# First layer's experts by unordered pairs: one sorted row a token, two experts a block

## The reference

```python
logits = xn @ gate_w + gate_b
tw, ti = jax.lax.top_k(logits, K)            # K = 2 of E = 6 experts
tw = jax.nn.softmax(tw, axis=-1)
w_full = jnp.sum(tw[..., None] * jax.nn.one_hot(ti, E, dtype=tw.dtype), axis=-2)
h = jax.nn.gelu(einsum('bsd,edh->besh', xn, ew1) + eb1, approximate=False)   # H = 256
eo = einsum('besh,ehd->besd', h, ew2) + eb2
moe = einsum('bse,besd->bsd', w_full, eo)
abel = gelu(xn @ aw1 + ab1) @ aw2 + ab2      # 128 -> 512 -> 128
nonabel = moe rotated by four expm(gens[i])
gate = sigmoid(concat([abel, nonabel]) @ gc_w + gc_b)
g = x + abel * (1 - gate) + nonabel * gate
```

## Time and profile before

| | us |
|---|---|
| median of 3 runs | 713.91 |
| lowest, highest | 711.11, 715.43 |
| the profiled execution | 718.61 |
| its span, first to last instruction | 716.9 |
| PE busy in the span | 626.8 |
| DVE busy | 496.5 |
| ACT busy | 415.2 |
| POOL busy | 447.6 |

### The profile page before, as it was taken

One profiled execution on the slowest core, in us unless ns is written; L12 is line 12 of the kernel. 1 busy time (PEld: TensorE's weight loads), 2 busy tenths in 40 slices (PEclk: granted clock), 3 DMA queues, 4 the chain that ended last, 5 costly groups with the idle time before them and its releaser, 6 DMA issues.

```text
span 716.9 us, 19568 instructions
## 1 busy us (share of the span) xinstructions
PE 626.8 (87%) x6221; PEld 443.8 (62%) x6222; DVE 496.5 (69%) x1302; ACT 415.2 (58%) x1144; POOL 447.6 (62%) x663
## 2 busy tenths in 40 slices
PE   4799889786876997896799999995999999999994
PEld 3667767686875865675354555554999845555442
DVE  5678776667665716998488888883444477887884
ACT  2575334443443454776666787773444367878793
POOL 7775888887068869974122476764333258878782
PEclk9999999999999999998999999998999999999997
DMA  8995111144566621110010000001222101111110
GB/s 230 289 301 149 42 45 56 56 113 87 104 114 127 128 56 33 31 24 13 1 32 2 8 32 24 24 28 35 69 70 70 56 21 42 32 32 31 32 46 16
DMA packets 69466, 48.34 MB, mean 67 GB/s; under 512 B 8011, under 2 KB 63750, under 8 KB 69382
## 3 DMA queue, kind: packets, MB, share of 16 engines
q1 hardware_dynamic: 62332, 34.09, 18.4%
q0 software_dynamic: 6144, 12.63, 7.3%
q10 hardware_dynamic: 906, 0.55, 0.3%
HBM read 24.00 MB, written 23.24 MB: 66 GB/s over the span
## 4 chain that ended last, share of the span: by engine, by line
PE 41%; POOL 23%; issue 17%; DVE 8%; DMA 5%; ACT 3%; SPq 1%; DVEq 0%; ACTq 0%; POOLq 0%
PE bank L1746 6%; PE bank L1817 5%; PE bank L1826 5%; POOL vs L1658 5%; POOL pool_xy L1056 5%; PE bank L1012 4%; DMA xg<-x_half 4%; PE bank L1726 3%; POOL xn_all L1634 3%; PE bank L1115 2%; POOL spacer L1051 2%; PE bank L1125 2%; DVE nmx L2058 2%; PE bank L579 2%; PE bank L1105 1%
## 5 line engine op out<-in xcount | busy, mean ns | idle before, releaser
L1891 ACT ACTIVATE pb<-bank,nmx 128x512 f32<-128x512 f32 x256 | 173.5, 691 | 65.5 <-DVE nmx L2058 62.6
L2058 DVE TENSOR_REDUCE nmx<-bank 128x2 f32<-128x1024 f32 x128 | 155.1, 1215 | 13.3 <-PE bank L1746 11.8
L1227 ACT ACTIVATE turns<-bank,cols 128x128 f32<-128x128 f32 x148 | 46.4, 364 | 65.5 <-PE bank L1115 41.4
L1658 POOL TENSOR_TENSOR vs<-vt_first,rz 128x256 f32<-128x256 f32 x64 | 39.4, 615 | 70.9 <-DVE rz L2034 69.9
L1726 PEld LDWEIGHTS bank<-pb,vs 128*32 128x32 f32 x2048 | 54.5, 110 | 37.6 <-issue 19.4
L1726 PE MATMUL bank<-pb,vs 128*32 128x128 f32 x2048 | 69.6, 275 | 2.0 <-POOL vs L1658 2.0
L382 POOL DMA_INDIRECT x_half<-pool_xy,slot x64 | 62.3, 973 | 10.6 <-issue 10.6
L1746 PE MATMUL bank<-qk 64*128 64x512 f32 x256 | 65.6, 622 | 1.6 <-ACT pb L1891 1.1
L1746 PE MATMUL bank<-qk_first 64*128 64x512 f32 x256 | 64.6, 619 | 2.2 <-ACT pb L1891 1.0
L1658 POOL TENSOR_TENSOR vs<-vt,rz 128x256 f32<-128x256 f32 x64 | 39.2, 615 | 36.5 <-DVE rz L2034 32.1
L1691 POOL COPY xn_all<-w 128x512 f32 x39 | 23.9, 615 | 51.3 <-PE bank L1817 49.2
(11 more groups left out here) (275 smaller groups left out, 1450.6 us busy)
## 6 DMA issues: line engine op xcount, KB each, us to landing
y_half<-ys SPq DMA_DIRECT2D x74, 64.5 KB
x_half<-zero SPq DMA_DIRECT2D x2, 2368.0 KB, 17.6
xg<-x_half SPq DMA_DIRECT2D x74, 64.0 KB
x_sorted<-zero SPq DMA_DIRECT2D x1, 2496.0 KB, 18.5
xn_all<-x_sorted SPq DMA_DIRECT2D x39, 64.0 KB, 1.8
y_sorted<-xn_all SPq DMA_DIRECT2D x39, 64.0 KB, 1.6
x_all<-in_L_attn_x_dram SPq DMA_DIRECT2D x8, 256.0 KB, 6.8
w<-in_L_ffn_W_dram SPq DMA_DIRECT2D x1, 2048.0 KB, 11.9
```

The costliest lines, as they stand in the source:

```text
L1658: pool.tensor_tensor(vs[s][:, :, :], vt[bt % 2][:, n // 2 % TT, :, :].rearrange("p j d -> p (j d)") .unsqueeze(1).broadcast_to([P, 2, D]), ...
L1891: act.activation(pb[s + ab][:, :], psum[score_banks(k) + ab], ACT.Exp, bias=nmx[:, s + ab:s + ab + 1], scale=1.0, accum_out=zz[:, s + ab:s ...
L2058: dve.tensor_reduce(nmx[:, s:s + 2], banks[:, score_banks(k):score_banks(k) + 2, :], AX.X, ALU.max, negate=True).then_inc(n_mx, 1)
```

## The change

A token has one class instead of two experts: the unordered pair of its experts, NC = 15. Each token is sorted once, into NB0 = 32 + 14 = 46 blocks; its row in the table is 130 wide, the 128 values and the two weights. DVE makes the classes as products of the two-hot rows, over all tokens at once: `ranks`, `offsets`, `first_blocks` and `slots` run once, in batches 4 and 5, on 15 x 32 = 480 values instead of twice on 96, and `block_experts` makes two expert numbers a block in batches 5 and 6. The two weights come from an exponential of ACT (`pair_weights`). POOL scatters 32 times, once the numbers, the weights and the zero fill are there. In a block, PE does four first and four second products, ACT four gelus, POOL (no longer DVE) copies the first weights of both experts, and DVE puts both biases, each scaled by its weight, into the result and adds both experts' halves out of the bank by their weights. In the mixing one row a token is gathered, all 32 behind the last block; the residual is added by DVE's first pass of `mix`, the dense part by its second, straight out of the banks, and ACT's `first_part` and POOL's `residual` are gone. In the second layer the scatters go one in two steps.

```diff
 NTH = NT // 2
-NBH = 2 * NTH + E0 - 1
-NB0 = 2 * NBH
+NC = E0 * (E0 - 1) // 2
+NB0 = NT + NC - 1
...
     def scatter(g):
-        for slot_w in (slot1, slot2):
-            pool.indirect_dma_start(
-                out=x_half[g // NTH], out_offset=bass.IndirectOffsetOnAxis(ap=slot_w[:, g:g + 1], axis=0),
-                in_=xh[:, g, :], in_offset=None).then_inc(t_sc0[g // NTH], 16)
-            space()
+        pool.indirect_dma_start(
+            out=x_pair, out_offset=bass.IndirectOffsetOnAxis(ap=slot0[:, g:g + 1], axis=0),
+            in_=xh[:, g, :], in_offset=None).then_inc(t_sc0, 16)
+        space()
...
-    for h in range(2):
-        pool.wait_ge(a_sl, h + 1)
-        pool.wait_ge(t_zf[h], 16)
-        for g in range(h * NTH, (h + 1) * NTH):
-            scatter(g)
+    pool.wait_ge(a_wt, 2)
+    pool.wait_ge(a_sl, 1)
+    pool.wait_ge(t_zf[0], 16)
+    for g in range(NT):
+        scatter(g)
...
-        dve.tensor_tensor(mo[:, :, :], oh1[:, half, :], oh2[:, half, :], ALU.add).then_inc(a_mo, 1)
...
+        dve.tensor_tensor(sg[:, half], sn[:, half], mt[:, :], ALU.is_gt)
+        step(dve.tensor_tensor(mo[:, :, :], oh1[:, half, :], oh2[:, half, :], ALU.add))
+        for a in range(E0 - 1):
+            n = E0 - 1 - a
+            last = dve.tensor_tensor(cls[:, FIRST_OF[a]:FIRST_OF[a] + n, half],
+                                     mo[:, :, a + 1:E0].rearrange("p t e -> p e t"),
+                                     mo[:, :, a].unsqueeze(1).broadcast_to([P, n, NTH]), ALU.mult)
+        last.then_inc(a_mo, 1)
...
+            dve.tensor_tensor(wp[:, :], sg[:, :], u[:, :], ALU.mult)
+            step(dve.tensor_tensor(wq[:, :], sn[:, :], v[:, :], ALU.mult))
+            dve.tensor_tensor(xh[:, :, D + i], wp[:, :], wq[:, :], ALU.add).then_inc(a_wt, 1)
+            dve.wait_ge(a_wt, i + 1)
...
-        for oh, slot_w in ((oh1, slot1), (oh2, slot2)):
-            step(dve.tensor_tensor(offo[:, :, :], off0[:, :, :], oh[:, half, :].rearrange("p t e -> p e t"),
-                                   ALU.mult))
-            step(dve.tensor_reduce(sl_f[:, :], offo[:, :, :].rearrange("p e t -> p t e"), AX.X, ALU.add))
-            last = dve.tensor_copy(slot_w[:, half], sl_f[:, :])
-            if oh is oh1:
+        step(dve.tensor_tensor(offo[:, :, :], off0[:, :, :], cls[:, :, :], ALU.mult))
+        step(dve.tensor_reduce(sl_f[:, :], offo[:, :, :].rearrange("p c t -> p t c"), AX.X, ALU.add))
+        dve.tensor_copy(slot0[:, :], sl_f[:, :]).then_inc(a_sl, 1)
...
             norm(1)
-        if bt - 1 in ROUTES:
-            slots(ROUTES.index(bt - 1))
+        if bt == ROUTES[1] + 1:
+            slots()
+            pair_weights()
         if bt in ROUTES:
             first_pick(ROUTES.index(bt))
...
+        both = expert(k)
+        if k >= NW:
+            pool.wait_ge(o_up, k - NW + 1)
+        for i in range(2):
+            pool.tensor_copy(wst0[k % NW][:, i * H0:(i + 1) * H0],
+                             w_e1[:, bass.ds(both[i], 1), :].rearrange("p a h -> p (a h)")).then_inc(o_w, 1)
+    def gather(g, alone=False):
+        pool.indirect_dma_start(
+            out=yg0[:, g, :], out_offset=None, in_=y_pair,
+            in_offset=bass.IndirectOffsetOnAxis(ap=slot0[:, g:g + 1], axis=0)).then_inc(f_yg[g // TT], 16)
+        if not alone:
             space()
...
-    for g in range(4):
-        gather(NTH + g)
-    for bt in range(1, B + 2):
-        first = 4 + (0, 2, 4, 6, 8, 9, 11)[bt - 1] if bt < B else NTH
-        if bt <= B:
-            residual(bt - 1)
-        if first < NTH:
-            gather(NTH + first)
-        if 2 <= bt:
-            power(bt - 2)
-        if first + 1 < NTH and bt != 5:
-            gather(NTH + first + 1)
+    for j in range(NY):
+        pool.wait_ge(o_st[j], 16 * ((NB0 - 1 - j) // NY + 1))
+    for g in range(2 * TT):
+        gather(g)
+    for bt in range(2, B + 2):
+        if bt < B:
+            gather(bt * TT)
+            gather(bt * TT + 1, True)
+        power(bt - 2)
+        if bt < B:
+            gather(bt * TT + 2)
+            gather(bt * TT + 3)
...
     def expert_down(k):
...
+        both = expert(k)
         pe.wait_ge(o_h, k + 1)
         if k > 1:
             pe.wait_ge(o_y, k - 1)
...
+        for i in range(2):
+            for c in range(EC):
+                mm = pe.matmul(psum[MBANK[k % 2]][:, i * DX:(i + 1) * DX],
+                               hT0[k % NW][:, (i * EC + c) * P:(i * EC + c + 1) * P],
+                               w_e2[:, bass.ds(both[i] * EC + c, 1), :].rearrange("p a d -> p (a d)"),
+                               start=(i == 0 and c == 0), stop=(c == EC - 1), skip_group_check=True)
...
-        if n == 2 and bt > 2:
+        if n == 3 and bt > 2:
             next_T(bt - 3)
         down(c)
-        if n == 3 and bt > 2:
-            next_scores(bt - 3)
+        if n == 0 and bt > 3:
+            next_scores(bt - 4)
+    next_scores(B - 4)
...
         gelu(bt * AC + 1)
+        if bt:
+            gate_tanh(bt - 1)
+        gelu(bt * AC + 2)
         if bt > 1:
             silu_tanh(bt - 2)
-        if bt:
-            gate_tanh(bt - 1)
...
-        gelu(bt * AC + 2)
         gelu(bt * AC + 3)
+        if bt + 1 < B:
+            gelu(bt * AC + 4)
         if bt > 2:
             next_store(bt - 3)
...
     def store_turned(k):
         dve.wait_ge(o_T, k + 1)
-        if 1 < k <= LEAD:
+        if k > 1:
             dve.wait_ge(o_up, k - 1)
...
+    def first_bias(k):
+        if k >= NY:
+            dve.wait_ge(o_st[k % NY], 16 * (k // NY))
+        dve.tensor_scalar(ys0[k % NY][:, :], bias_of(expert(k)[0]), weight_of(k, 0), None, ALU.mult).then_inc(o_b1, 1)
+    def second_bias(k):
+        dve.wait_ge(o_b1, k + 1)
+        dve.scalar_tensor_tensor(ys0[k % NY][:, :], bias_of(expert(k)[1]), weight_of(k, 1), ys0[k % NY][:, :],
+                                 ALU.mult, ALU.add).then_inc(o_b2, 1)
+    def first_expert(k):
         dve.wait_ge(o_dn, k + 1)
-        if k >= NB0 - LEAD:
-            dve.wait_ge(o_st[k % NY], 16 * (k // NY))
-        dve.tensor_tensor(ys0[k % NY][:, :], psum[MBANK[k % 2]][:, 0:DX],
-                          b2x[:, bass.ds(e, 1), :].rearrange("p a d -> p (a d)"), ALU.add).then_inc(o_y, 1)
-    copy_weight(0)
+        dve.wait_ge(o_b2, k + 1)
+        dve.scalar_tensor_tensor(ys0[k % NY][:, :], psum[MBANK[k % 2]][:, 0:DX], weight_of(k, 0), ys0[k % NY][:, :],
+                                 ALU.mult, ALU.add).then_inc(o_f1, 1)
+    def second_expert(k):
+        dve.wait_ge(o_f1, k + 1)
+        dve.scalar_tensor_tensor(ys0[k % NY][:, :], psum[MBANK[k % 2]][:, DX:2 * DX], weight_of(k, 1), ys0[k % NY][:, :],
+                                 ALU.mult, ALU.add).then_inc(o_y, 1)
...
     for i in range(NB0 + LEAD):
-        expert(i + 2)
+        expert(i)
+        if 0 <= i - 2 < NB0:
+            first_bias(i - 2)
         if i < NB0:
             store_turned(i)
-        if i + 1 < NB0:
-            copy_weight(i + 1)
         if i >= LEAD:
-            finish_block(i - LEAD)
-    dve.wait_ge(f_th, 1)
-    dve.tensor_scalar(w2t[:, :], th[:, :], 0.5, 0.5, ALU.mult, ALU.add)
-    step(dve.tensor_scalar(w1t[:, :], th[:, :], -0.5, 0.5, ALU.mult, ALU.add))
+            first_expert(i - LEAD)
+        if 0 <= i - 2 < NB0:
+            second_bias(i - 2)
+        if i >= LEAD:
+            second_expert(i - LEAD)
...
+        dve.wait_ge(f_yg[bt], 16 * TT)
+        if bt:
+            dve.wait_ge(f_gt, bt)
         dve.wait_ge(f_dn, (bt + 1) * AC)
-        dve.tensor_tensor(gz[:, 0:3], gz[:, 0:3], a[:, 0:3 * DX].rearrange("p (t d) -> p t d", t=3)[:, :, D], ALU.add)
-        dve.tensor_tensor(gz[:, 3:4], gz[:, 3:4], b_[:, D:DX], ALU.add).then_inc(f_gz, 1)
...
+        dve.tensor_tensor(gz[:, 0:3], yg0[:, bt * TT:bt * TT + 3, D],
+                          a[:, 0:3 * DX].rearrange("p (t d) -> p t d", t=3)[:, :, D], ALU.add)
+        dve.tensor_tensor(gz[:, 3:4], yg0[:, bt * TT + 3, D:DX], b_[:, D:DX], ALU.add).then_inc(f_gz, 1)
...
-        dve.wait_ge(f_r0, bt + 1)
+        a, b_ = (psum[i] for i in ABANKS[bt % 2])
+        dve.wait_ge(f_gg, bt + 1)
+        dve.wait_ge(f_xa, bt + 1)
         for t in range(TT):
-            y = in_half(bt * TT // NTH, bt * TT + t)
-            ins = dve.scalar_tensor_tensor(r[:, t, :], y[:, 0, 0:D], gw1[:, t:t + 1], r[:, t, :], ALU.mult, ALU.add)
+            ins = dve.scalar_tensor_tensor(r[:, t, :], yg0[:, bt * TT + t, 0:D], gg[bt % 2][:, t:t + 1],
+                                           xn_all[:, bt * TT + t, :], ALU.mult, ALU.add)
         step(ins)
         for t in range(TT):
-            y = in_half(bt * TT // NTH, bt * TT + t)
-            ins = dve.scalar_tensor_tensor(r[:, t, :], y[:, 1, 0:D], gw2[:, t:t + 1], r[:, t, :], ALU.mult, ALU.add)
+            mine = a[:, t * DX:t * DX + D] if t < 3 else b_[:, 0:D]
+            ins = dve.scalar_tensor_tensor(r[:, t, :], mine, og[bt % 2][:, t:t + 1], r[:, t, :], ALU.mult, ALU.add)
```

(22 more changed lines are left out.)

288 lines of the change are left out of this document (135 added, 153 removed).

## The result

| | before | with the change |
|---|---|---|
| median, us | 714.67 (4 runs, 711.11 to 716.12) | 741.12 (4 runs, 737.61 to 744.82) |
| the profiled execution, us | 718.61 | 737.61 |
| its span, us | 716.9 | 735.9 |

The ratio is 1.0357, with a 95% interval of 1.0306 to 1.0407: the change costs 3.6%, and the forecast of 741.0 lies on the median. (The forecast started from 713.9, the median of three of these four runs of the kernel before.) How much of that is luck the stages tell. The execution profiled with the change lies 3.5 under its median, the one of before 3.9 over its own, so the two traces are only 19.0 us apart and not 26.5.

A forecast was written before the change was run, and what follows sets the result against it. No engine was full in the experts' stretch; scatters and the mixing's chain were the other places to see. Start +14.9, blocks −7.9, mixing +22.8, second layer −3.0: +26.8 on 713.9 gives 741, range 733 to 750.

The forecast's parts named there:

- Start of the blocks: Scatters and POOL's queue ahead of the experts' stretch: PE's first product at 155.4 instead of 140.51, +14.9 us.
- its cover: What the routing adds to the attention, some 7 us at most, hides behind POOL; the attention ends near 146.
- The blocks: Experts' stretch: 46 blocks at 2.15 us, bounds 2.0 and 2.5, plus irregular time; they give back 7.9 us.
- irregular time: Experts' stretch, beyond quiet blocks and gelu's table: 10.7 us before, 46/74 of it, 6.6, with the change.
- the ring: Blocks: the load of block k+3 waits for block k−3's finish; 6.7 us for three blocks, 2.2 each.
- rival A: Quick blocks: 2.0 us each and irregular time 3 instead of 6.6; total 730, chance 0.18.
- Rival B, the lock: Blocks: DVE stands while POOL copies from SBUF, one copy a block; pace 2.5 us, +16, total 757, chance 0.12.
- The mixing: Two gathers enter the chain behind the power: cycles of 12.3, then 13.6 us; 22.8 us arise here.
- Rival C: Mixing: gathers don't bind, 73.9 us to last gate sums kept, 3 more for late first gathers; 721, chance 0.04.
- the landing: Mixing: a gather's landing taken as 1.7 us, bounds 1.2 and 2.5, six times over −3 to +5.
- The second layer: Its first block: −4.6 without the wait for the last scatter, +1.6 for denser scatters' hold-ups; together −3.0 us.
- The sum: Whole kernel: +29.8 − 3.0 = +26.8 us; 745.4 for the profiled execution's like, 741 for the median.

The follow-up runs named there:

- both orders: The kernel after with the gathers ahead of the power and POOL's weight copies ahead of its bias additions; 725.62 us, ratio 1.0108.
- all edits: Kernel after with gathers ahead of power, mix ahead of gate sums, copies ahead of bias additions, seven row buffers, turned rows ahead of first bias; 696.45 us, 0.9761.
- the kernel before with sparse scatters: The kernel before with only the second layer's scatters changed, one in two steps instead of three in eight; 708.56 us, ratio 0.9935.
- without spacers: The kernel after without the memset on POOL behind each of the first layer's 32 scatters; 772.49 us, ratio 1.0741.
- the short one: The kernel with all edits, the memset behind each first-layer scatter 96 columns wide instead of 384; 726.56 us, ratio 1.0122.

## Why the prediction was right, and where not

**Start of the blocks: right, its cover mis-sized.** +16.7 instead of +14.9: POOL began 1.3 later, and the last scatter was 2 later. The wait for POOL's copies came as worked out. But the text put all that the routing adds to the attention at 7 us at most. It was 12.7, from 138.47 to 151.22. It arises in three batches: DVE stores v (L880 before, L927 with the change) 0.3 us later in batch 4, and then 4.5, 8.8 and 12.8 later in batches 5, 6 and 7. DVE's routing instructions (L776 to L835 before, L795 to L876 with the change) grew from 18.0 to 24.9 us; some stand ahead of the copies of probabilities that PE waits for (3.4 us before 112.1, 2.8 before 133.2), and PE's mean clock between the first scatter and the end of the attention was 0.93, where before it was 1.00. How the 12.7 divide between the instructions and the clock isn't known. In the kernel after this cost nothing, since POOL was later. It did cost in the profiles of both orders and of all edits, where POOL was early and the attention ended at 156.9 and 156.8.

**The blocks: the mean turn as forecast, the sum 6.4 too high.** Turns came 2.14 apart in the mean, forecast 2.15, and 46 × 2.14 and gelu's table of 1.3 make 99.7 of the 100.4. But this mean holds every stall. The forecast took 2.15 for a quiet block, as the earlier trace rows gave 1.32, and put 6.6 us of irregular time on top. Read in the same way, the seven quietest blocks with the change take 14.3 us, 2.04 each:

```profile
181.10 0.33 PE L1144 MATMUL bank<-ident,xg_all 128*128 128x128 f32 x1 [0.81 <-DMA xg_all<-x_pair]
...
195.40 0.33 PE L1144 MATMUL bank<-ident,xg_all 128*128 128x128 f32 x1
```

46 × 2.04 make 93.8, and 5.3 are left as irregular time. (The split is loose: the quietest seven blocks of the kernel before took 8.8 us and not the 9.2 of the earlier trace rows.) So what was mis-sized is mostly the quiet pace, by 0.11 a block or 5.1 us, and the irregular time by 1.3; the ring, given as the reason for 2.15, stretches only some of the blocks. The whole, 100.4, lies between the forecast's 106.8 and rival A's 96.3 (46 × 2.0, 3 and 1.3): A had the quiet pace, the forecast the irregular time. And the ring was one of two reasons: DVE's order at the handover, which the text didn't have, gives nearly the same mean.

How much the blocks give back depends on the execution of the kernel before: the same code took 114.7 us in its profile and 106.0 in the profile of the kernel before with sparse scatters (first product 143.06, mixing 249.07). Against that second profile the blocks give back 5.6 us, against the first 14.3, and the forecast's 7.9 lies between.

**Rival B, the lock: it didn't set the pace, since the two hardly meet.** DVE's second bias took 0.35 us in the mean, where B's sign was 0.5, and POOL was busy for 34.14 of the 100.4 us:

```profile
L1376 DVE SCALAR_TENSOR_TENSOR ys<-b2x,xg_all,ys 128x129 f32<-128x129 f32 x46 | 16.0, 348 | 0.1
```

In that trace one of the 46 second biases overlaps a copy of POOL, and this one took 0.48 us. But what B describes can be seen in the kernel with the copies ahead of the additions, where a bias addition of POOL (L1108) lies in a block:

```profile
161.24 1.27 POOL L1108 TENSOR_TENSOR xn_all<-xn_all,ab_bc 128x512 f32<-128x512 f32 x1
...
161.57 1.09 DVE L1380 SCALAR_TENSOR_TENSOR ys<-b2x,xg_all,ys 128x129 f32<-128x129 f32 x1
```

The second bias took 1.09 us instead of 0.35 and ended 0.15 behind POOL's addition; the other two that met such an addition there took 1.09 as well. It costs little since the two meet so seldom, which is the reason that the prediction gave against B.

**The mixing: right.** Gate sums of batch 1 at +17.8 (forecast 17.7), two cycles of 12.3 (12.3), four of 13.7 to 14.4 (13.6): 98.4 us, against 96.7. What is missing in the sum is mainly the growth of the last cycles with the falling clock, 1.7 in all. Rival C is refuted: the gathers bind, and with them out of the chain 18 us go, where C differed by 20. The prediction didn't have the next bound, PE's banks held until the mix, which costs another 14 once the gathers are away. Of the landing: The Trainium skill, DMA: Bandwidth & Descriptors, section on the anatomy of one DMA, gives about 2.0 us of fixed cost for a transfer from POOL's queue. Here a gather took 2.55 from issue to landing with its own descriptors, and 1.6 without, so the figure lies between the two; the chain is fed by the whole 2.55.

**The second layer: the size right, its parts not.** Alone, in the kernel before, this part gained 5.3, where −4.6 and +1.6 were put: the 4.6 was near, and nothing is seen of the 1.6. In the kernel after the same stretch is 3.7 shorter, near the forecast's 3.0. Why 1.6 less isn't settled, and one profile can't settle it: in the seven other profiles with the gate sums in the change's order this stretch, whose code is the same, took 163.2 to 166.3 us, from 3.0 us under the kernel before to none. So the nearness of 3.7 to 3.0 is in part luck.

**The sum.** +16.7, −14.3, +24.5 and −3.7 make +23.2 between the two traces at the second layer's first product, and +19.0 at the end, for in the last stretch, whose code is the same, the trace of before was 4.2 slower. Between the medians it is +26.5. The difference is probably that the trace of before is of a long execution: with the second profile of that code in the first layer, +14.1, −5.6, +22.7 and −3.7 make +27.5. By the first profile the start and the mixing cost 1.8 and 1.7 more than forecast, and the blocks and the second layer gave back 6.4 and 0.7 more. That the forecast lies on the median is therefore luck in part: the mechanism of each stage was in the main as told, but its errors of size lie on both sides.

## What to carry to other kernels

Write down the cycle before moving a wait: the loss was not in the pairing of experts, which saves transfers and even block time, but in two gathers placed behind a power that waits for the batch before them, and in gate sums placed ahead of a mix that frees PE's banks. Reordering those lines of two queues turned +3.6% into −0.9%, and three smaller edits made it −2.4%. And when near-equal bounds lie side by side, as in the blocks, an experiment that removes one and shows nothing doesn't clear it. A mean pace also already holds the stalls: before irregular time is added to it, a pace has to be read from quiet blocks.

## What was not expected of the hardware

Indirect scatters that follow each other on POOL every 1.27 or 1.33 us brought DVE and ACT to a stand for up to 30 us; every 1.57 us they didn't. Some of these waits ended while the scatters were still running (DVE at 119.27, ACT at 131.27 without spacers), the longest only behind the last scatter (ACT at 146.97 without spacers, DVE at 143.78 with the short one). What they wait for no run here shows. The mixing's instructions ran, in different orders, with a mean granted clock between 0.83 and 1.00: at 1.00 where PE idled 2 to 7 us of the stretch, at 0.92 to 0.98 where it idled 12, and at 0.83 to 0.86 where it idled 17 to 19, though not in strict order, for the kernel after idled most (19.4 us) and had 0.86.
